# Rounded rows of the split chunks written a second time, into a PSUM bank, in the first gather of a two-layer graph network

## The chip, the cores and the metric

The kernel runs on one core of one Trainium2 chip. The metric is the device time of one execution in microseconds. The core's engines work in parallel, each on its own list of instructions: TensorE (PE), VectorE (DVE), ScalarE (ACT), GpSimd (POOL) and SyncE (SP). They are ordered among each other only by semaphores.

## The reference, cut to what matters

Two graph layers with residual and layer norm over 6,250 nodes of 512 features, with 100,000 edges sorted by destination. Layer 0 is the one that the change touches:

```python
agg = segment_sum(x[src], dst, num_segments=N)     # 6250 x 512
h = (1.0 + eps) * x + agg
h = relu(batch_norm(h @ W1 + b1, g1, be1))         # 512 -> 1024
h = relu(batch_norm(h @ W2 + b2, g2, be2))         # 1024 -> 512
x = layernorm(x + x + h)
```

Layer 1 gathers again over the same edges, with one weight of 512 x 512. All of it is float32.

## The kernel before, in words

The program has five phases: gather 0 (aggregation and the first product of layer 0), the hidden phase (second product), the rows phase (norms), gather 1, and rows again. The change lies in `gather_phase`, which builds both gathers; `layer` says which.

**The gather.** The edges are 782 chunks of 128. For each chunk GpSimd issues one indirect DMA (line 542) that fetches 128 rows of 512 floats from HBM into one slot of `ring`, which has 34 slots in layer 0. The nodes are 50 tiles of 125, handled as 25 pairs (h is 0 or 1 in a pair). A tile takes a window of 18 chunks; neighbouring windows overlap, so a pair needs 782/25 = 31.3 new chunks. SyncE counts landed chunks into the semaphore `landed` (line 518). GpSimd waits for `used` before it overwrites slots.

**The aggregation.** `scatter` on TensorE multiplies, for each chunk of the window, a 0/1 matrix (`select`, which VectorE compares into being in `selection`) with the rows of the chunk, and adds into the tile's PSUM bank. Ten places of the 18 are "whole": float32 operands, two passes (line 767, two records each). Eight places are "split": ScalarE copies the rows from `ring` into `rows_hi[:, k]` rounded to fp32r (line 854, `high_rows`), VectorE subtracts that from the rows and has the low part `rows_lo[:, k]` (line 638, `low_rows`), and TensorE multiplies both, high (line 752) and low (line 757). k is 0 to 7, and each of the eight has a buffer of its own, so ScalarE may run up to eight rows ahead of VectorE, and both ahead of TensorE. TensorE takes whole and split places alternately. The order of the list is fixed:

```python
order = whole[:1]
for k, p in enumerate(whole[1:]):
    order += [p] + split[k:k + 1]
```

**The semaphores of a split row.** `split_hi` counts finished rows of ScalarE, VectorE waits for it; `split_lo` counts finished low parts, TensorE waits for it; `split_used` counts rows that TensorE has consumed, and ScalarE waits for it before it writes buffer k again.

**The rest of a pair.** VectorE forms `sums` = own rows + PSUM bank once a tile is finished (line 653, `read_sums`). TensorE transposes the sums (`turn`), ScalarE rounds them (line 845, `high_part`), VectorE takes the low part (line 661, `low_part`), and TensorE makes the product with W1 in four pieces (line 795, `product`), pushed in between the places of the next pair's tiles: piece 0 after the ninth place of tile 0, piece 1 behind its last, pieces 2 and 3 after the sixth and twelfth place of tile 1. ScalarE reads each piece out of PSUM (line 865, `read_product`), VectorE takes its statistics (line 669). VectorE's and ScalarE's lists for a pair are written out by hand:

```python
read_sums(v, tiles(pair, 1), 1)
low_rows(v, 0, first[0], 0, 2)
low_part(v)
low_rows(v, 0, first[0], 2, 5)
selection(v, 1, tiles(i, 1), first[1])
low_rows(v, 0, first[0], 5, SPLIT)
read_sums(v, tiles(i, 0), 0)
low_rows(v, 1, first[1], 0, 4)
```

and so on. PSUM has eight banks: 0 and 1 hold the tiles' sums, 2 and 3 the transposed, 4 and 5 the products, 6 `column_ps`, and 7 counts edges in layer 1; in layer 0 it is free after the set-up.

Of the kernel before, what the change touches and what calls it, by code (L numbers as in the profile page):

```python
# [4 lines left out]
F32 = mybir.dt.float32  # L5
F32R = mybir.dt.float32r
# [3 lines left out]
ALU = mybir.AluOpType  # L10
ACT = mybir.ActivationFunctionType
# [359 lines left out]
def gather_phase(nc, z, m, layer):  # L371
# [12 lines left out]
    SPLIT = z.SPLIT[layer]  # L384
    WINDOW = z.WINDOW
    SPLIT_AT, ORDER = z.split_places(layer), z.order(layer)
# [19 lines left out]
    with ExitStack() as ctx:  # L406
# [11 lines left out]
        rows_hi, rows_lo = sb("rows_hi", [P, SPLIT, z.D], F32R), sb("rows_lo", [P, SPLIT, z.D], F32R)  # L418
# [21 lines left out]
        split_hi = sem("split_hi")  # L440
        split_lo = sem("split_lo")
# [26 lines left out]

        turn_ps = m.banks(2, 4)
        prod_ps = m.banks(4, 6)  # L470
        count_ps = m.bank(7)

        def tiles(i, h):
            return 2 * i + h
# [7 lines left out]
        def within(engine, value, most, why):  # L482
            return nc.s_assert_within(engine.snap(value), 0, most, skip_runtime_bounds_check_because=why)

        def of_use(engine, i, groups, g):
            return within(engine, i * groups + g, USES - 1, "i and g count below the pairs and the groups")

        def first_chunk(engine, tile, g):

            first = engine.value_load(m.first[:, bass.ds(tile, 1)], min_val=0, max_val=z.CHUNKS - WINDOW)  # L490
            return within(engine, first + g * z.STRIDE, z.CHUNKS - WINDOW + 1, "first is 0 unless there is but one group")

        def of_chunk(engine, first, place):

            at = within(engine, (first + place) % S * z.D, (S - 1) * z.D, "a slot of the ring")
            return ring[:, bass.ds(at, z.D)]
# [9 lines left out]
        with nc.Block(name=f"gather{layer}") as block:  # L506
# [79 lines left out]
            def _(dve):  # L586
                nc.vector.sem_inc(lo_done, 1)
                nc.vector.sem_inc(stats_done, 1)
                if layer == 0:
                    setup.vector(dve)  # L590
                groups = dve.value_load(m.groups, min_val=1, max_val=z.ALL_GROUPS)
# [43 lines left out]
                def low_rows(v, h, first, a, b):  # L635
                    for k in range(min(a, SPLIT), min(b, SPLIT)):
                        dve.wait_ge(split_hi, SPLIT * (2 * v + h) + k + 1)
                        nc.vector.tensor_tensor(rows_lo[:, k, :], of_chunk(dve, first, SPLIT_AT[k]),  # L638
                                                rows_hi[:, k, :].bitcast(F32), ALU.subtract).then_inc(split_lo, 1)

                def read_sums(reads, tile, h):

# [42 lines left out]
                with dve.Fori(0, z.PAIRS) as i:  # L685
                    with dve.Fori(0, groups) as g:
                        v = of_use(dve, i, groups, g)
                        pair = dve.snap(before, min_val=0, max_val=z.PAIRS - 1)
                        first = [first_chunk(dve, tiles(i, h), g) for h in range(2)]
# [32 lines left out]
            def _(pe):  # L722
# [10 lines left out]
                def agg(h):  # L733
                    return m.bank(h)[0:z.NT, :]
# [6 lines left out]
                def scatter(i, v, g, tile, h):  # L741
                    tile_use = pe.snap(2 * v + h)
                    first = first_chunk(pe, tile, g)

                    begin = pe.snap(i * per_pair + first + 1)
                    pe.wait_ge(sums_done[h], v + 1)
                    pe.wait_ge(select_done[h], 2 * v + 2)
                    for n, p in enumerate(ORDER):
                        if p in SPLIT_AT:
                            k = SPLIT_AT.index(p)  # L750
                            pe.wait_ge(split_lo, SPLIT * tile_use + k + 1)
                            high = nc.tensor.matmul(agg(h), select_r[h][:, k, :], rows_hi[:, k, :], start=False,  # L752
                                                    stop=False, skip_group_check=True)

                            if n % 2:
                                high.then_inc(used, 1)
                            nc.tensor.matmul(agg(h), select_r[h][:, k, :], rows_lo[:, k, :], start=False,  # L757
                                             stop=False, skip_group_check=True).then_inc(split_used, 1)
                        else:
                            if n + 1 == WINDOW and layer == 1:  # L760
                                pe.wait_ge(counted[h], v + 1)
                                for c in range(2):
                                    nc.tensor.matmul(count_ps[0:z.NT, bass.ds(tile, 1)], edge_count[h][:, c, :],
                                                     m.ones[:, 0:1], start=False, stop=c == 1, skip_group_check=True)
                            place = last_place if p + 1 == WINDOW else p
                            pe.wait_ge(landed, begin + place)
                            whole = nc.tensor.matmul(agg(h), select[h][:, WHOLE_AT.index(p), :], of_chunk(pe, first, place),  # L767
                                                     start=False, stop=n + 1 == WINDOW, skip_group_check=True)
                            if n % 2:
                                whole.then_inc(used, 1)  # L770
                        if n + 1 in PRODUCT_AT[h]:
                            product(v, PRODUCT_AT[h][n + 1])
# [36 lines left out]
                with pe.Fori(0, z.PAIRS) as i:  # L809
                    clear(i, 0)  # L810
                    clear(i, 1)
                    with pe.Fori(0, groups) as g:
                        v = of_use(pe, i, groups, g)
                        turn(v)
                        scatter(i, v, g, tiles(i, 0), 0)
                        scatter(i, v, g, tiles(i, 1), 1)
# [6 lines left out]
            def _(act):  # L823
# [26 lines left out]
                def high_rows(i, v, h, first, a, b):  # L850
                    for k in range(min(a, SPLIT), min(b, SPLIT)):
                        act.wait_ge(split_used, SPLIT * (2 * v + h) + k + 1)
                        act.wait_ge(landed, i * per_pair + first + (SPLIT_AT[k] + 1))
                        nc.scalar.activation(rows_hi[:, k, :], of_chunk(act, first, SPLIT_AT[k]), ACT.Copy  # L854
                                             ).then_inc(split_hi, 1)

                def read_product(job, pair, b, store=True):
                    if layer == 0 and b == 0:
# [29 lines left out]
                with act.Fori(0, z.PAIRS) as i:  # L888
                    with act.Fori(0, groups) as g:
                        v = of_use(act, i, groups, g)  # L890
                        pair = act.snap(before, min_val=0, max_val=z.PAIRS - 1)
                        first = [first_chunk(act, tiles(i, h), g) for h in range(2)]
# [478 lines left out]
def gnn_kernel(nc, x, src, dst, eps, w1, b1, g1, be1, w2, b2, g2, be2, w3, b3, g3, be3, out):  # L1371
# [7 lines left out]
    with ExitStack() as ctx:  # L1379
# [54 lines left out]
        with ExitStack() as third:  # L1434
            m.w3_hi = sb("w3_hi", [P, z.KD, z.D], F32R, scope=third)
            m.w3_lo = sb("w3_lo", [P, z.KD, z.D], F32R, scope=third)
            m.stats3 = sb("stats3", [P, z.KD, z.PAIRS * 6], scope=third)
            gather_phase(nc, z, m, 1)
# [22 lines left out]
```

## Time and profile before

| | |
|---|---|
| median of 3 runs | 2598.41 us (2590.33 to 2599.28) |
| profiled execution | 2596.4 us, its span 2594.7 us |
| first gather (tiles) | 42 us to 1060 us of the span |
| second gather (tiles) | 1491 us to 2480 us |
| TensorE busy, share of the span | 2309.4 us, 89% |
| GpSimd busy | 1604.1 us, 62% |
| VectorE busy | 1361.8 us, 52% |
| ScalarE busy | 796.0 us, 31% |
| mean granted TensorE clock | 0.942 of full |

Busy time is the sum of an engine's instructions. TensorE's ends are modelled and include time in which a matmul stands in the pipeline. The share over the span mixes phases: GpSimd has nothing to do from 1053 us to 1400 us, and in both gathers it is the other way round. A group's mean duration and a single row's duration are both used below; "x3" in a row means three like instructions in one stretch, whose time runs from the first start to the last end.

### The profile page before, as it was taken

What the parts mean: (1) busy time and instruction counts of PE and PEld (TensorE: products, weight loads), DVE (VectorE), ACT (ScalarE), POOL (GpSimd) and SP (SyncE); (2) the same over time, 40 slices, a digit from 0 to 9 for tenths busy, and PEclk for the clock granted to TensorE, in tenths of its full rate; (3) what the DMA queues carried; (4) which work ended last, traced back from release to release, by engine and by line L of the source; (5) the groups of instructions that cost most, each with busy time, mean ns of one, the idle gap of its engine ahead of it and who ended that gap; (6) DMA issues with size and microseconds to landing.
All of it is one profiled execution on the core that took longest, in us unless ns stands there. A gap on an engine that the chain in (4) does not pass through costs nothing. (4 is left out here: it accounts for less than half of the span.)

```text
span 2594.7 us, 41691 instructions
## 1 busy us (share of the span) xinstructions
PE 2309.4 (89%) x9657; PEld 1514.8 (58%) x9658; DVE 1361.8 (52%) x2155; ACT 796.0 (31%) x1272; POOL 1604.1 (62%) x1729
## 2 busy tenths in 40 slices
PE   3999999999999999799995299999999999999964
PEld 2666666666666666688884255555555555555544
DVE  5555555555555455433336655545545555554557
ACT  1233333333333333455548411111111111111147
POOL 6777777777777777100002467777777777777712
PEclk9999999999999999899996699999999999999976
DMA  7777777777777777332217767777777777777748
GB/s 254 221 237 241 224 246 237 231 242 218 242 240 231 247 223 248 101 111 93 89 55 228 254 190 219 212 226 217 224 222 213 222 222 215 225 224 215 224 136 286
DMA packets 180571, 545.11 MB, mean 210 GB/s; under 512 B 48787, under 2 KB 51178, under 8 KB 175794
## 3 DMA queue, kind: packets, MB, share of 16 engines
q0 software_dynamic: 125120, 410.09, 53.3%
q1 hardware_dynamic: 33880, 78.23, 10.0%
q10 hardware_dynamic: 21544, 56.48, 6.5%
q8 instruction: 10, 0.16, 0.0%
q14 instruction: 17, 0.14, 0.0%
HBM read 493.06 MB, written 51.62 MB: 210 GB/s over the span
## 5 line engine op out<-in xcount | busy, mean ns | idle before, releaser
L767 PE MATMUL psum<-ring,select 128*125 x2600 | 1272.5, 613 | 12.3 <-issue 8.6
L542 POOL DMA_INDIRECT ring<-x_in,staged x782 | 799.2, 1022 | 249.7 <-issue 223.7
L542 POOL DMA_INDIRECT ring<-x_d,staged x782 | 750.2, 959 | 261.7 <-issue 223.0
L767 PEld LDWEIGHTS psum<-ring,select 128*125 128x125 f32 x2600 | 483.5, 192 | 383.6 <-issue 338.2
L638 DVE TENSOR_TENSOR rows_lo<-ring,rows_hi 128x512 fp32r<-128x512 f32 x500 | 327.5, 688 | 281.2 <-ACT rows_hi L854 279.3
L854 ACT ACTIVATE rows_hi<-ring 128x512 fp32r x500 | 289.4, 623 | 418.2 <-SPq L518 282.1
L795 PE MATMUL psum<-sumsT_hi,w_hi 128*128 128x250 f32 x1248 | 401.1, 321 | 4.3 <-DVE sumsT_lo L661 4.3
L752 PE MATMUL psum<-rows_hi,select_r 128*125 128x512 f32 x500 | 380.9, 762 | 7.1 <-DVE rows_lo L638 3.6
L795 PE MATMUL psum<-sumsT_lo,w_hi 128*128 128x250 f32 x1248 | 350.5, 281 | 0.0
L795 PE MATMUL psum<-sumsT_hi,w_lo 128*128 128x250 f32 x1248 | 348.9, 280 | 0.0
L795 PEld LDWEIGHTS psum<-sumsT_hi,w_hi 128*128 128x128 f32 x1248 | 237.9, 191 | 36.0 <-issue 32.6
L795 PEld LDWEIGHTS psum<-sumsT_lo,w_hi 128*128 128x128 f32 x1248 | 239.2, 192 | 30.9 <-issue 29.9
L795 PEld LDWEIGHTS psum<-sumsT_hi,w_lo 128*128 128x128 f32 x1248 | 239.2, 192 | 0.0
L1268 POOL TENSOR_TENSOR both_r<-six_r 125x5 f32<-125x5 f32 x18 | 3.6, 199 | 377.2 <-DVE six_r L1331 377.2
L649 DVE TENSOR_SCALAR lone<-psum 125x1 f32 (+1 forms) x51 | 8.0, 158 | 420.5 <-PE psum L767 420.5
L868 ACT ACTIVATE h3T<-psum,vecs 128x250 f32 (+1 forms) x104 | 43.1, 465 | 568.8 <-PE psum L795 568.8
L865 ACT ACTIVATE hidden<-psum,vecs 128x250 f32<-128x250 f32 x208 | 86.1, 466 | 388.1 <-PE psum L795 388.0
L632 DVE TENSOR_REDUCE edge_count<-select 128x125 bf16<-128x2000 f32 x51 | 202.3, 3967 | 0.0
L757 PE MATMUL psum<-rows_lo,select_r 128*125 128x512 f32 x500 | 199.2, 398 | 0.0
L752 PEld LDWEIGHTS psum<-rows_hi,select_r 128*125 128x125 f32 x500 | 97.3, 195 | 141.2 <-issue 89.5
L1105 PE MATMUL psum<-act_hi,w_hi 128*128 128x500 f32 (+1 forms) x416 | 159.9, 384 | 11.9 <-DVE act_lo L1063 11.9
L1299 PE MATMUL psum<-ident,normed_r 128*125 128x128 f32 x400 | 89.4, 415 | 83.6 <-ACT normed_r L1221 83.6
(161 smaller groups left out, 2257.0 us busy)
## 6 DMA issues: line engine op xcount, KB each, us to landing
hidden_d<-hidden ACTq DMA_DIRECT2D x25, 1000.0 KB
act_f<-hidden_d SPq DMA_DIRECT2D x24, 1000.0 KB
ring<-x_in,staged POOLq DMA_INDIRECT x782, 3.8
ring<-x_d,staged POOLq DMA_INDIRECT x782, 3.7
own<-x_in ACTq DMA_DIRECT2D x50, 224.0 KB
own_r<-x_in SPq DMA_DIRECT2D x10, 1120.0 KB
own<-x_d ACTq DMA_DIRECT2D x50, 224.0 KB
own_r<-x_d SPq DMA_DIRECT2D x10, 1120.0 KB
```

The source lines that it names most:

```text
L542: nc.gpsimd.indirect_dma_start(slot(s), None, table, bass.IndirectOffsetOnAxis(ap=staged[:, s:s + 1], axis=0)).then_inc(gathered[s], 16)
L632: nc.vector.tensor_reduce(edge_count[h][:, 1, :], select[h][:].rearrange("p k n -> p n k"), AX.X, ALU.add).then_inc(counted[h], 1)
L638: nc.vector.tensor_tensor(rows_lo[:, k, :], of_chunk(dve, first, SPLIT_AT[k]), rows_hi[:, k, :].bitcast(F32), ALU.subtract).then_inc(split ...
L752: high = nc.tensor.matmul(agg(h), select_r[h][:, k, :], rows_hi[:, k, :], start=False, stop=False, skip_group_check=True)
L757: nc.tensor.matmul(agg(h), select_r[h][:, k, :], rows_lo[:, k, :], start=False, stop=False, skip_group_check=True).then_inc(split_used, 1)
L767: whole = nc.tensor.matmul(agg(h), select[h][:, WHOLE_AT.index(p), :], of_chunk(pe, first, place), start=False, stop=n + 1 == WINDOW, skip ...
L795: last = nc.tensor.matmul(out, w[:, k, o * P:(o + 1) * P], s[:, k, :], start=n == 0, stop=n == len(parts) - 1)
L854: nc.scalar.activation(rows_hi[:, k, :], of_chunk(act, first, SPLIT_AT[k]), ACT.Copy).then_inc(split_hi, 1)
L865: nc.scalar.activation(hidden[:, o, :], from_, ACT.Identity, bias=m.b1[:, o:o + 1]).then_inc(out_done, 1)
L868: nc.scalar.activation(m.h3T[:, o, bass.ds(pair * z.W, z.W)], from_, ACT.Relu, bias=m.b3[:, o:o + 1]).then_inc(out_done, 1)
L1105: last = nc.tensor.matmul(out, w[:, f * KK + k, o * P:(o + 1) * P], s[:, 0:pairs, k, :] if pairs == 2 else s[:, 0, k, :], start=f == 0 and ...
L1299: last = nc.tensor.transpose(m.bank(n % BANKS)[0:z.NT, k * P:(k + 1) * P], normed[i % 2][:, k, u, :], m.ident[:])
```

## The change: what it does

In layer 0 ScalarE makes each rounded row twice: once into `rows_hi` as before, and once more, with the same source, into PSUM bank 7 (`high_ps`). VectorE's subtraction takes the rounded rows from bank 7 in place of `rows_hi`. Since there is one bank and not eight, ScalarE now also waits, before each row, until VectorE has done the row before (`split_lo`). That semaphore starts at 1 in both layers, and TensorE's waits on it go up by 1 to match. Layer 1 keeps its instructions.

```diff
         turn_ps = m.banks(2, 4)
         prod_ps = m.banks(4, 6)
-        count_ps = m.bank(7)
+
+        high_ps = count_ps = m.bank(7)
...
                 nc.vector.sem_inc(lo_done, 1)
                 nc.vector.sem_inc(stats_done, 1)
+                nc.vector.sem_inc(split_lo, 1)
...
                         dve.wait_ge(split_hi, SPLIT * (2 * v + h) + k + 1)
-                        nc.vector.tensor_tensor(rows_lo[:, k, :], of_chunk(dve, first, SPLIT_AT[k]),
-                                                rows_hi[:, k, :].bitcast(F32), ALU.subtract).then_inc(split_lo, 1)
+                        high = high_ps if layer == 0 else rows_hi[:, k, :].bitcast(F32)
+                        nc.vector.tensor_tensor(rows_lo[:, k, :], of_chunk(dve, first, SPLIT_AT[k]), high, ALU.subtract
+                                                ).then_inc(split_lo, 1)
...
-                            pe.wait_ge(split_lo, SPLIT * tile_use + k + 1)
+                            pe.wait_ge(split_lo, SPLIT * tile_use + k + 2)
...
                         act.wait_ge(split_used, SPLIT * (2 * v + h) + k + 1)
+                        if layer == 0:
+
+                            act.wait_ge(split_lo, SPLIT * (2 * v + h) + k + 1)
                         act.wait_ge(landed, i * per_pair + first + (SPLIT_AT[k] + 1))
-                        nc.scalar.activation(rows_hi[:, k, :], of_chunk(act, first, SPLIT_AT[k]), ACT.Copy
-                                             ).then_inc(split_hi, 1)
+                        high = nc.scalar.activation(rows_hi[:, k, :], of_chunk(act, first, SPLIT_AT[k]), ACT.Copy)
+                        if layer == 0:
+                            high = nc.scalar.activation(high_ps.bitcast(F32R), of_chunk(act, first, SPLIT_AT[k]), ACT.Copy)
+                        high.then_inc(split_hi, 1)
```

What stands on ScalarE for one split row of layer 0, in the loop over pairs, before the change (names in brackets are the semaphores that the instruction waits for; ISA and REGISTER_ALU rows compute a wait's value or an address):

```order
L852 REGISTER_ALU
L853 REGISTER_ALU [waits gather0_split_used]
L854 ISA [waits gather0_landed]
L854 ACTIVATE rows_hi<-ring 128x512
L859 ISA
```

The same place of ScalarE's list after it:

```order
L855 REGISTER_ALU
L859 REGISTER_ALU [waits gather0_split_lo,gather0_split_used]
L860 ISA [waits gather0_landed]
L860 ACTIVATE rows_hi<-ring 128x512
L862 ACTIVATE psum<-ring 128x512
```

One ACTIVATE per row is added behind the old one, and the row's first wait has a second semaphore. On VectorE the list keeps its length; between the tiles of a pair it reads, before:

```order
L638 TENSOR_TENSOR rows_lo<-ring,rows_hi 128x512
L644 REGISTER_ALU [waits gather0_own_in0]
L645 REGISTER_ALU [waits gather0_used]
L653 SCALAR_TENSOR_TENSOR sums_0<-own_0,self_weight,psum 125x512 [waits gather0_turned]
L637 ISA
L638 ISA [waits gather0_split_hi]
L638 TENSOR_TENSOR rows_lo<-ring,rows_hi 128x512
```

and after, at the same place:

```order
L641 TENSOR_TENSOR rows_lo<-ring,psum 128x512
L647 REGISTER_ALU [waits gather0_own_in0]
L648 REGISTER_ALU [waits gather0_used]
L656 SCALAR_TENSOR_TENSOR sums_0<-own_0,self_weight,psum 125x512 [waits gather0_turned]
L639 ISA
L641 ISA [waits gather0_split_hi]
L641 TENSOR_TENSOR rows_lo<-ring,psum 128x512
```

Nothing is moved on VectorE; only the second operand of the subtraction is another.

## Rows read from the trace of the kernel before

**Rows 1.** Busy tenths of GpSimd in 40 slices of the span, from the page.

```profile
POOL 6777777777777777100002467777777777777712
```

**Rows 2.** Groups of instructions, 88 to 1060 us: count, busy us, mean ns, idle before.

```profile
L542 POOL DMA_INDIRECT ring<-x_in,staged x725 | 742.8, 1025 | 223.0 <-issue 207.5 <-PE psum L767 13.7 <-DMA staged<-src_tab 1.8
...
L638 DVE TENSOR_TENSOR rows_lo<-ring,rows_hi 128x512 fp32r<-128x512 f32 x384 | 251.9, 687 | 264.9 <-ACT rows_hi L854 262.9 <-issue 1.7
...
L854 ACT ACTIVATE rows_hi<-ring 128x512 fp32r x384 | 220.4, 623 | 281.2 <-SPq L518 154.7 <-issue 90.6 <-ACT hidden L865 21.0
...
L661 DVE TENSOR_TENSOR sumsT_lo<-psum,sumsT_hi 128x500 fp32r<-128x500 f32 x48 | 30.2, 670 | 4.4 <-ACT sumsT_hi L845 4.3
...
L845 ACT ACTIVATE sumsT_hi<-psum 128x500 fp32r<-128x500 f32 x48 | 25.5, 583 | 11.2 <-PE psum L781 11.0
```

**Rows 3.** The sums instruction: count, durations, first and last start, 80 to 1070 us.

```profile
L653 DVE SCALAR_TENSOR_TENSOR sums<-own,self_weight,psum x49: 746/747/749, 88.4 to 1060.4; 125x512 f32<-125x512 f32 x49
```

**Rows 4.** The same groups in layer 1, 1600 to 2400 us.

```profile
L542 POOL DMA_INDIRECT ring<-x_d,staged x631 | 604.9, 959 | 195.6 <-issue 179.9 <-PE psum L767 12.7 <-DMA staged<-src_tab 3.0
...
L638 DVE TENSOR_TENSOR rows_lo<-ring,rows_hi 128x512 fp32r<-128x512 f32 x80 | 52.1, 691 | 0.0
```

**Rows 5.** Timeline of GpSimd: start us, duration us, instruction, idle before it.

```profile
604.76 0.95 POOL L542 DMA_INDIRECT ring<-x_in,staged  x1 [0.30 <-PE psum L767]
606.01 1.84 POOL L542 DMA_INDIRECT ring<-x_in,staged  x1 [0.30 <-issue]
...
619.49 1.43 POOL L542 DMA_INDIRECT ring<-x_in,staged  x1 [0.30 <-issue]
...
1052.36 0.95 POOL L542 DMA_INDIRECT ring<-x_in,staged  x1 [0.30 <-issue]
```

**Rows 6.** Timeline of VectorE in one pair.

```profile
605.76 1.27 DVE L638 TENSOR_TENSOR rows_lo<-ring,rows_hi 128x512 fp32r<-128x512 f32 x2
...
612.86 0.75 DVE L653 SCALAR_TENSOR_TENSOR sums<-own,self_weight,psum 125x512 f32<-125x512 f32 x1 [2.90 <-PE psum L767]
...
618.82 1.89 DVE L638 TENSOR_TENSOR rows_lo<-ring,rows_hi 128x512 fp32r<-128x512 f32 x3 [1.16 <-ACT rows_hi L854]
...
623.62 0.68 DVE L638 TENSOR_TENSOR rows_lo<-ring,rows_hi 128x512 fp32r<-128x512 f32 x1
```

**Rows 7.** Who waited for whom, 88 to 1060 us: total us, times, longest us.

```profile
PEld psum L752 <- DVE rows_lo L638: 22.8, 81, 1.3
```

**Rows 8.** Timeline of ScalarE and its queue in the same pair.

```profile
601.80 0.83 ACT L865 ACTIVATE hidden<-psum,vecs 128x250 f32<-128x250 f32 x2 [4.27 <-PE psum L795]
603.02 1.67 ACT L854 ACTIVATE rows_hi<-ring 128x512 fp32r x3 [0.39 <-ACT hidden L865]
...
614.16 1.15 ACT L854 ACTIVATE rows_hi<-ring 128x512 fp32r x2 [4.77 <-issue]
...
616.10 1.55 ACTq L839 DMA_DIRECT2D own<-x_in  x3
617.98 2.19 ACT L854 ACTIVATE rows_hi<-ring 128x512 fp32r x4 [1.58 <-SPq L518]
```

**Rows 9.** Timeline of TensorE without the product's matmuls, same pair.

```profile
604.71 1.02 PE L767 MATMUL psum<-ring,select 128*125 x2
...
608.37 0.40 PE L752 MATMUL psum<-rows_hi,select_r 128*125 128x512 f32 x1
...
608.61 0.39 PE L757 MATMUL psum<-rows_lo,select_r 128*125 128x512 f32 x1
...
608.84 1.02 PE L767 MATMUL psum<-ring,select 128*125 x2
...
611.48 1.02 PE L767 MATMUL psum<-ring,select 128*125 x2
```

**Rows 10.** One pair's stretch: length; busy PE, PEld, DVE, ACT, POOL; granted clock, DMA share, GB/s.

```profile
128.00:169.00 41.00, 39.00 (x180) 26.36 (x179) 21.46 (x38) 13.26 (x26) 31.56 (x32) 0.96 0.78 238
```

## The prediction

> **What bounds the kernel now.** I read the slices first: GpSimd is evenly busy through both gathers and idle between them [rows 1]. Then the groups of the stretch in which layer 0's tiles run. GpSimd issued 725 gathers with a mean of 1.025 us and 223.0 us of idle between them, 0.308 us each [rows 2]; together 1.333 us, and 725 x 1.333 = 966 us of the 972 us in the window. It never really rests: 207.5 us of that idle are "issue", the fixed 0.30 us in front of every row [rows 5]. The last gather starts at 1052.4 us [rows 5], 8 us before the last sums of the phase at 1060.4 us. So GpSimd's issue sets the pace of gather 0. A pair of tiles takes (1060.4 - 88.4)/24 = 40.5 us [rows 3]; TensorE shows 39.00 busy of 41.00 [rows 10], so it is a close second.
>
> The timeline of GpSimd shows what a gather costs: most rows last 0.94 to 0.95 us, some 1.43 or 1.84 [rows 5]. The long ones begin while VectorE is in the subtraction of line 638: 606.01 in 605.76 to 607.03, 619.49 in 618.82 to 620.71 [rows 5, 6]. In layer 1, where a window has two split rows and not eight, the mean is 0.959 us [rows 4]. So in layer 0 about 725 x (1.025 - 0.946) = 57 us of GpSimd's time is lengthening beside that subtraction (0.946 being the usual row).
>
> The Trainium skill, "SBUF — State Buffer", section "Who interferes with whom", says that a VectorE instruction with two SBUF inputs contends with a GpSimd instruction that reads SBUF; the trace agrees. In the same section it infers that `tensor_tensor` does not starve descriptor generation, by which the long rows would not exist and the change could give nothing; there the trace disagrees, 1.84 us against 0.95.
>
> **What the change does, part by part.** Layer 0 has 25 x 16 = 400 split rows.
>
> *Removed:* the second SBUF operand of VectorE's subtraction. If that frees GpSimd wholly, a gather costs 0.946 + 0.308 = 1.254 us, and GpSimd could do a pair in 31.3 x 1.254 = 39.2 us.
>
> *Added:* 400 copies on ScalarE, at 0.62 us each 248 us [rows 2]. ScalarE is busy 13.26 of 41 us in a pair [rows 10]; with 16 x 0.62 more it is at 23. As mere work this is covered by its idle time.
>
> *Added:* the wait. This is the term that decides. With one bank, row k+1 may be written only after VectorE has subtracted row k. Before, VectorE did three rows in 1.89 us [rows 6], because ScalarE had run ahead. Now each row is a handshake, of length h:
> - both copies of ScalarE, back to back: 1.15 us, the row of two such copies [rows 8]. The write into PSUM is not in the trace; below, two starts are never closer than (2.19 - 0.62)/3 = 0.52, so 1.04 for both; above, I allow 0.2 more. I take 1.15, since reading PSUM (583 ns for 500 columns) costs ScalarE about what SBUF does (623 for 512).
> - from ScalarE's end to VectorE's start: ScalarE's first of four ends at 617.98 + 0.62 = 618.60, VectorE starts at 618.82 [rows 6, 8]: 0.22.
> - the subtraction: 0.69. With one operand in PSUM the nearest is line 661, 670 ns for 500 columns [rows 2], no dearer.
> - back from VectorE to ScalarE: no such row. TensorE follows VectorE by some 0.06. ScalarE's own step from a finished DMA issue (616.10 + 1.55 = 617.65) over three address steps to its next start at 617.98 is 0.33 [rows 8]; two of these steps lie behind the new wait. 0.06 + 0.22 = 0.28, taken as 0.30; bounds 0.20 and 0.40.
>
> Sum: h = 1.15 + 0.22 + 0.69 + 0.30 = 2.36 us. Sixteen of them are 37.8 us, which alone is near the pair's 40.5; but in five places of a pair the step from one subtraction to the next is longer than h, because other work lies in it:
> - two selections on VectorE, which lie between two subtractions: the third of the three at 618.82 starts at 620.02, the next one at 623.62 [rows 6]: 3.60 each. ScalarE's next row is ready by then.
> - two tile ends. VectorE's `read_sums` waits for TensorE's last place, and that for the last low part: 0.69 (subtraction) + 0.06 + 1.49 (split pair and whole place, 608.37 to 608.84 + 1.02) [rows 9] + 0.36 (whole place over at 612.50, sums at 612.86) [rows 6, 9] + 0.68 (the sums' 0.75 less the usual overlap) = 3.28 each.
> - one `high_part` with the four DMA issues of `load_own` on ScalarE: from the start of a pair of copies at 614.16 to the next copy at 617.98 [rows 8]: 3.82.
>
> Everything else hides: statistics (1.4 us) and `low_part` fit into the 1.67 us that VectorE idles in each handshake; a `read_product` (1.22 us from start to next copy [rows 8]) fits beside the selections or in ScalarE's idle 1.2 us. The five replace five of the 16:
>
> pair = 11 h + 2 x 3.60 + 2 x 3.28 + 3.82 = 11 h + 17.6 = 26.0 + 17.6 = **43.6 us**.
>
> This loop closes over ScalarE, VectorE and, at tile ends, two places of TensorE; nothing in it waits for GpSimd. It is longer than 40.5, so the pace passes from GpSimd to this loop, and what GpSimd gains becomes idle time (waits on `used`). What is queued behind ScalarE's new wait: the later copies, `high_part`, the reads of the products. TensorE, which waited 22.8 us in the whole window for low rows [rows 7], would wait some 1 us at each split row of tile 0: it uses one per 1.3 us and gets one per 2.36.
>
> 24 periods x (43.6 - 40.5) = +74 us. The first pair and layer 1 I leave as they are (layer 1 has the same instructions). Profiled execution: 2596.4 + 74 = 2670; the median of the runs is 2.0 us above that execution: 2672.
>
> The Trainium skill, "VectorE: DVE Perf Modes", section on the TRN2 errata, charges VectorE 62 cycles more for a PSUM source than for SBUF, 65 ns at 0.96 GHz; by that estimate h grows to 2.43 and the time to about 2689. Line 661 reads PSUM and SBUF in 670 ns and shows none of it, so it stays out of the sum.
>
> **Range.** h from 2.20 (each term at its shorter side: 1.10, 0.20, 0.68, 0.22) to 2.65 (a copy into PSUM 0.15 dearer, return 0.40, the rest a little over) gives pairs of 41.8 to 46.8 and +31 to +151 us: 2629 to 2749. All lower bounds at once (1.04 + 0.20 + 0.67 + 0.20 = 2.11) give 40.8, no change.
>
> **The rivals.**
> - *The release wins (faster).* If h were short, GpSimd's pace would still count, at up to 57 us less; with TensorE near its limit (39 of 41 busy) about 24 x 1.5 = 36 to 57: 2540 to 2562. The deciding point is h = (40.5 - 17.6)/11 = 2.08 for equality and 1.96 for the 39.2 of a free GpSimd. For it: the contention is real. Against: three of four terms are measured and make 2.06 without the return. Only if copies overlap with VectorE's work in a way the loop excludes could it be. Chance 0.07.
> - *No change.* h near 2.08 to 2.15, or the loop's extra waits less than I count. 2590 to 2611. Chance 0.08.
> - *The loop plus a slower TensorE (slower still).* The granted clock is 0.96 in a pair's stretch [rows 10], 1.2 GHz for a part of it and 2.4 GHz for the rest. Waits of 1 us at most split rows may bring more time at 1.2 GHz. The sensitive place is piece 1 of the product: at full clock a piece takes about 2.9 us (605.5 to 608.37 [rows 9]), and ScalarE reads it just as it would start the next copy; at half clock it is 2.9 us late and so are all later rows. +2.9 per pair on top is 24 x 2.9 = 70: 2742. Chance 0.20.
> - *GpSimd isn't relieved* (rows stay at 1.025): 31.3 x 1.333 = 41.7 is still under 43.6, so the time is the forecast's. It is contained in it.
>
> **How the numbers follow.** The forecast, the handshake at h 2.2 to 2.65 with the clock as it is, has 0.65, its own range 2629 to 2749. The range of 2618 to 2745 leaves out the faster rival, most of no change, and the upper part of the clock's case. About 0.5% (13 us) is what a measurement of this kernel can tell from nothing. Faster 0.07; same 0.08; slower 0.85.
>
> **What the profile after should show.** GpSimd's gathers in layer 0 at a mean near 0.95 us, with more idle before them, now for TensorE. ScalarE with 400 more instructions. The subtraction still at 0.68 to 0.69 us, its starts 2.3 to 2.4 us apart inside a run, where they were 0.60. Sums 43 to 44 us apart for a pair. TensorE waiting for `rows_lo` by some 4 to 5 us a pair. Layer 1 unchanged in length. The prediction is wrong if the subtraction's starts are under 2.1 us apart, if ScalarE's write to PSUM is much quicker or dearer than 0.62, or if the clock falls for longer.

## The result: 5.8% slower

| | before | after |
|---|---|---|
| median, same comparison | 2595.23 us | 2746.52 us (2745.96 to 2749.34, 4 runs) |
| ratio to before | | 1.0578, 95% interval 1.056 to 1.0595 |
| profiled span | 2594.7 us | 2744.4 us |
| last sums of gather 0 start at | 1060.4 us | 1212.1 us |
| mean granted TensorE clock | 0.942 | 0.936 |

The sign and the mechanism were those forecast. The size was not: +151 us against +74, and 2746.5 lies 1.5 us outside the stated range of 2618 to 2745. All of it is in gather 0: its last sums come 151.7 us later, and everything behind it takes the same time to within 2 us.

Each ratio below compares a kernel with the kernel before in the same set of runs, and the kernel before took 2590 to 2596 us in some sets and 3067 to 3133 us in others, called slow sets here, for a reason that is not known (the expectations put it down to the chip, but chip 4 of the record shows both).

The sums of the changed kernel, from 80 to 1200 us and to 1230 us (count, durations, first and last start), which answer to [rows 3]:

```profile
L656 DVE SCALAR_TENSOR_TENSOR sums<-own,self_weight,psum x48: 746/748/749, 95.2 to 1190.8; 125x512 f32<-125x512 f32 x48
L656 DVE SCALAR_TENSOR_TENSOR sums<-own,self_weight,psum x49: 746/748/750, 95.2 to 1212.1; 125x512 f32<-125x512 f32 x49
```

(1212.1 - 95.2)/24 = 46.5 us a pair, where it was 40.5. The first sums, too, come 6.8 us later (95.2 against 88.4).

The page's groups of the changed kernel, which answer to [rows 2], for the whole of gather 0 (the L755 row counts both gathers, 400 and 100):

```profile
L543 POOL DMA_INDIRECT ring<-x_in,staged x782 | 740.6, 947 | 426.7 <-issue 216.3
...
L641 DVE TENSOR_TENSOR rows_lo<-ring,psum 128x512 fp32r<-128x512 f32 x400 | 274.5, 686 | 480.1 <-ACT psum L862 480.1
...
L755 PEld LDWEIGHTS psum<-rows_hi,select_r 128*125 128x125 f32 x500 | 96.2, 192 | 281.1 <-DVE rows_lo L641 222.1
...
L862 ACT ACTIVATE psum<-ring 128x512 fp32r x400 | 233.2, 583 | 0.0
```

GpSimd's gathers fell to 947 ns: the lengthening is gone. But its idle time rose to 426.7 us. VectorE now waits 480 us for ScalarE's write into PSUM, and TensorE waits for low rows (next table).

Who waited for whom in the changed kernel, 100 to 1190 us (total us, times, longest us):

```profile
DVE rows_lo L641 <- ACT psum L862: 444.8, 305, 1.8
ACT rows_hi L860 <- DVE rows_lo L641: 262.8, 205, 2.3
...
POOL ring L543 <- PE psum L770: 195.9, 90, 9.1
PEld psum L755 <- DVE rows_lo L641: 180.4, 191, 1.6
...
DVE sums L656 <- issue: 73.9, 23, 3.5
...
DVE local L611 <- issue: 15.1, 23, 0.7
```

The first two rows are the handshake, each engine waiting for the other. The third says that GpSimd waits for TensorE, 195.9 us where it was 13.7 [rows 2]. The fourth is TensorE's wait for low rows, 180.4 us or 7.7 a pair, where 4 to 5 were forecast. The last two were not forecast. 73.9 us in 23 times is 3.2 us a pair in which VectorE stood before its sums and waited for no engine; 15.1 us is 0.66 a pair before a selection.

### The profile page after: what moved, and what is told of

It reads as the page before. It is cut to its first block and busy times, and to the rows that moved or that the text cites. A ratio compares the mean times of both kernels' runs of the same rounds, so it can differ in the third digit from the quotient of the medians.

```text
span 2744.4 us, 42493 instructions
## 1 busy us (share of the span) xinstructions
PE 2355.6 (86%) x9657; PEld 1511.0 (55%) x9658; DVE 1372.9 (50%) x2155; ACT 1008.3 (37%) x1672; POOL 1545.2 (56%) x1729
## 5 line engine op out<-in xcount | busy, mean ns | idle before, releaser
L543 POOL DMA_INDIRECT ring<-x_in,staged x782 | 740.6, 947 | 426.7 <-issue 216.3
L860 ACT ACTIVATE rows_hi<-ring 128x512 fp32r x500 | 312.7, 630 | 737.7 <-DVE rows_lo L641 286.2
L641 DVE TENSOR_TENSOR rows_lo<-ring,psum 128x512 fp32r<-128x512 f32 x400 | 274.5, 686 | 480.1 <-ACT psum L862 480.1
L755 PE MATMUL psum<-rows_hi,select_r 128*125 128x512 f32 x500 | 335.0, 670 | 61.5 <-DVE rows_lo L641 58.0
L755 PEld LDWEIGHTS psum<-rows_hi,select_r 128*125 128x125 f32 x500 | 96.2, 192 | 281.1 <-DVE rows_lo L641 222.1
L862 ACT ACTIVATE psum<-ring 128x512 fp32r x400 | 233.2, 583 | 0.0
```

The source lines that it names most:

```text
L543: nc.gpsimd.indirect_dma_start(slot(s), None, table, bass.IndirectOffsetOnAxis(ap=staged[:, s:s + 1], axis=0)).then_inc(gathered[s], 16)
L860: high = nc.scalar.activation(rows_hi[:, k, :], of_chunk(act, first, SPLIT_AT[k]), ACT.Copy)
L862: high = nc.scalar.activation(high_ps.bitcast(F32R), of_chunk(act, first, SPLIT_AT[k]), ACT.Copy)
```

## Where a pair's 46.8 us go

Timeline of VectorE in the changed kernel, cut from one pair. Where a row shows no idle time before it, VectorE came to it straight from other work:

```profile
609.29 0.69 DVE L641 TENSOR_TENSOR rows_lo<-ring,psum 128x512 fp32r<-128x512 f32 x1 [0.90 <-ACT psum L862]
611.71 0.69 DVE L641 TENSOR_TENSOR rows_lo<-ring,psum 128x512 fp32r<-128x512 f32 x1 [1.73 <-ACT psum L862]
...
614.91 0.69 DVE L641 TENSOR_TENSOR rows_lo<-ring,psum 128x512 fp32r<-128x512 f32 x1 [1.34 <-ACT psum L862]
617.23 0.69 DVE L641 TENSOR_TENSOR rows_lo<-ring,psum 128x512 fp32r<-128x512 f32 x1 [1.63 <-ACT psum L862]
619.53 0.69 DVE L641 TENSOR_TENSOR rows_lo<-ring,psum 128x512 fp32r<-128x512 f32 x1 [1.61 <-ACT psum L862]
...
623.15 0.68 DVE L641 TENSOR_TENSOR rows_lo<-ring,psum 128x512 fp32r<-128x512 f32 x1
...
627.75 0.69 DVE L641 TENSOR_TENSOR rows_lo<-ring,psum 128x512 fp32r<-128x512 f32 x1 [1.62 <-ACT psum L862]
630.21 0.75 DVE L656 SCALAR_TENSOR_TENSOR sums<-own,self_weight,psum 125x512 f32<-125x512 f32 x1 [1.77 <-PE psum L770]
630.88 0.68 DVE L641 TENSOR_TENSOR rows_lo<-ring,psum 128x512 fp32r<-128x512 f32 x1
...
637.79 0.69 DVE L641 TENSOR_TENSOR rows_lo<-ring,psum 128x512 fp32r<-128x512 f32 x1 [1.61 <-ACT psum L862]
639.14 0.30 DVE L611 TENSOR_SCALAR local<-dst_t,tile_bases 128x17 f32 x1 [0.66 <-issue]
...
642.19 0.68 DVE L641 TENSOR_TENSOR rows_lo<-ring,psum 128x512 fp32r<-128x512 f32 x1
...
649.12 0.69 DVE L641 TENSOR_TENSOR rows_lo<-ring,psum 128x512 fp32r<-128x512 f32 x1 [1.63 <-ACT psum L862]
...
654.43 0.75 DVE L656 SCALAR_TENSOR_TENSOR sums<-own,self_weight,psum 125x512 f32<-125x512 f32 x1 [3.33 <-issue]
656.11 0.69 DVE L641 TENSOR_TENSOR rows_lo<-ring,psum 128x512 fp32r<-128x512 f32 x1 [0.93 <-ACT psum L862]
```

From start to start of the subtraction, in us:

| step | forecast | measured |
|---|---|---|
| handshake (617.23 to 619.53), 11 of them | 2.36 | 2.31 |
| first selection (619.53 to 623.15) | 3.60 | 3.62 |
| second selection (637.79 to 642.19) | 3.60 | 4.40 |
| end of tile 0 (627.75 to 630.88) | 3.28 | 3.13 |
| `high_part` (611.71 to 614.91) | 3.82 | 3.20 |
| end of tile 1, over the loop's turn (649.12 to 656.11) | 3.28 | 6.99 |
| a pair | 43.6 | 11 x 2.31 + 21.3 = 46.8 |

The pair shown takes 656.11 - 609.29 = 46.8 us, a little more than the mean of 46.5. What happens in the last step stands in the sequencers' own records: the instructions that load registers, which the profile does not count as busy. They are here with start, duration and end in us (not a view of the profile):

```
650.969 0.903 -> 651.872 Vector TENSOR_LOAD L491
651.125 1.055 -> 652.180 Scalar TENSOR_LOAD L491
652.294 1.496 -> 653.790 Vector TENSOR_LOAD L491
652.564 1.261 -> 653.825 Scalar TENSOR_LOAD L491
654.429 0.747 -> 655.176 Vector SCALAR_TENSOR_TENSOR L656
654.594 0.629 -> 655.223 Scalar ACTIVATE L860
```

At the head of the loop both engines load `first`, the number of a tile's first chunk, for the two tiles of the pair out of SBUF into registers. TensorE's last place of tile 1 ended at 650.43 + 1.02 = 651.45, and by the forecast the sums would have followed at 651.8; they start at 654.43. ScalarE's first copy can't start before its own loads are through either, so the next subtraction waits for it once more (0.93). The step before the second selection holds a load of the same kind, 0.32 us long in VectorE's records.

## The experiments

The edits are shown against the changed kernel, unless the text says otherwise.

**relief_only.** Against the kernel before: VectorE's one SBUF operand less, without copies or handshake. VectorE subtracts a constant that a memset left in bank 7; the low parts are not the reference's.

```diff
-                        if layer == 0:
-                            act.wait_ge(split_lo, SPLIT * (2 * v + h) + k + 1)
...
-                        if layer == 0:
-                            high = nc.scalar.activation(high_ps.bitcast(F32R), of_chunk(act, first, SPLIT_AT[k]), ACT.Copy)
...
+                if layer == 0:
+                    dve.wait_ge(setup.vecs_done, 1)
+                    nc.vector.memset(m.bank(7), 0.0)
```

> The changed kernel without ScalarE's second copy and without its new wait; VectorE subtracts what a memset left in bank 7 (so the low parts are not those of the reference). It asks what VectorE's one SBUF operand less is worth by itself. Theory of the handshake (the new loop between ScalarE and VectorE made all of the +151 us, the second operand relieves GpSimd): gathers of layer 0 at a mean of 0.946 us, pairs at 39 to 39.5 us, 2540 to 2570 us. Rival (GpSimd's gathers aren't what paces layer 0): about 2595 us. Rival (a PSUM operand makes VectorE late): above 2600 us.

In a slow set: 1.0054 (1.0024 to 1.0084). Again:

> relief_only once more, since the chip of its first run took 3070 us for the kernel before, with gathers that landed later, and could not tell the kernels apart. The changed kernel without the second copy and without the new wait; VectorE subtracts what a memset left in bank 7. On a chip where the kernel before takes about 2598 us: theory of the handshake 2540 to 2570 us, gathers at 0.946 us; rival (GpSimd does not pace layer 0) about 2595 us.

Measured: 2598.23 us against 2595.02, ratio 1.0006 (0.9982 to 1.003). GpSimd in relief_only_again, 88 to 1040 us:

```profile
L543 POOL DMA_INDIRECT ring<-x_in,staged x724 | 686.6, 948 | 253.6 <-issue 206.2 <-PE psum L773 47.1 <-DMA staged<-src_tab 0.3
```

The relief is complete (948 ns) and brings nothing beyond 0.3% either way; pairs still take (1059.4 - 88.2)/24 = 40.5 us. The last gather starts at 1026.4 us, 33 us before the last sums, where it was 8: GpSimd ran ahead and nothing followed. The handshake theory was right that this operand is the cause of the long gathers, and wrong about what they are worth. In the kernel before, GpSimd was not what held the pace. The rival's 2595 us is what came. One of the ten runs took 2573.3 us, with a granted clock of 0.951 where the others had 0.939 to 0.943; why isn't known.

**copy_only.** The 400 copies without the handshake.

```diff
-                            act.wait_ge(split_lo, SPLIT * (2 * v + h) + k + 1)
+                            act.wait_ge(split_hi, SPLIT * (2 * v + h) + k)
...
-                        high = high_ps if layer == 0 else rows_hi[:, k, :].bitcast(F32)
+                        high = rows_hi[:, k, :].bitcast(F32)
```

> The changed kernel with the second copy into bank 7, but VectorE subtracts rows_hi as before, and ScalarE waits only for its own previous copy instead of VectorE's subtraction. Theory of the handshake: 400 more copies fit into ScalarE's idle time, pairs at 40.5 to 41 us, 2590 to 2615 us. Rival (the work of the copies itself makes the time): 2680 to 2750 us.

In a slow set. Twice again:

> copy_only on a chip where the kernel before takes about 2595 us: the second copy into bank 7 stays, VectorE subtracts rows_hi as before, and ScalarE waits only for its own previous copy. Theory of the handshake: 400 more copies fit into ScalarE's idle time, 2590 to 2620 us. Rival (the work of the copies itself makes the time): 2680 to 2750 us.

> copy_only on a chip where the kernel before takes about 2595 us: second copy kept, VectorE subtracts rows_hi, ScalarE waits only for its own previous copy. Theory of the handshake: 2590 to 2620 us. Rival (the work of the copies itself): 2680 to 2750 us.

All three fell in slow sets: 1.0078 (1.005 to 1.0105), 1.0043 (1.0012 to 1.0074), 1.0053 (1.002 to 1.0086). There the copies cost 0.4 to 0.8%. There is no run of this kernel beside one of 2590 to 2596 us; psum_first, which has the same copies, bounds their cost there.

**wait_only.** The handshake without the second copy (`rows_hi` is VectorE's operand again).

```diff
-                        high = high_ps if layer == 0 else rows_hi[:, k, :].bitcast(F32)
+                        high = rows_hi[:, k, :].bitcast(F32)
...
-                        if layer == 0:
-                            high = nc.scalar.activation(high_ps.bitcast(F32R), of_chunk(act, first, SPLIT_AT[k]), ACT.Copy)
```

> The changed kernel with its new wait, but without the second copy, and with VectorE subtracting rows_hi. The handshake is then one copy shorter: 2.31 - 0.54 = 1.77 us. Theory of the handshake, with the loop turn counted: 11 x 1.77 + 3.6 + 4.4 + 3.1 + 6.4 + 2.7 = 39.7 us a pair, just under GpSimd's pace of 40.5, so 2590 to 2640 us, VectorE's starts 1.8 us apart in a run. Rival (it is the wait as such, whatever its length): near 2746 us.

In a slow set 1.0086 (1.0055 to 1.0118). Again:

> wait_only once more, for the same reason: the new wait without the second copy, VectorE subtracts rows_hi. Theory of the handshake with h = 1.77 us: 2590 to 2640 us. Rival (the wait as such, whatever its length): near 2746 us.

Measured: 2615.6 us against 2595.02, ratio 1.0082 (1.0065 to 1.0099). A handshake of 1.8 us costs 0.8%, not 5.8. Its pairs take (1081.2 - 89.9)/24 = 41.3 us, where 39.7 were expected from the loop alone. Its gathers stay long, 1018 ns on average.

**psum_first.** All the work of the change, but bank 7 is written first and releases VectorE; `rows_hi` is written beside VectorE's subtraction.

```diff
+                            nc.scalar.activation(high_ps.bitcast(F32R), of_chunk(act, first, SPLIT_AT[k]), ACT.Copy
+                                                 ).then_inc(split_hi, 1)
+                        nc.scalar.activation(rows_hi[:, k, :], of_chunk(act, first, SPLIT_AT[k]), ACT.Copy
+                                             ).then_inc(hi_stored if layer == 0 else split_hi, 1)
...
                             pe.wait_ge(split_lo, SPLIT * tile_use + k + 2)
+                            if layer == 0:
+                                pe.wait_ge(hi_stored, SPLIT * tile_use + k + 1)
```

> The changed kernel with ScalarE's two copies in the other order: bank 7 first, which releases VectorE, then rows_hi, beside VectorE's subtraction; TensorE waits for rows_hi by a semaphore of its own. All the work of the change is kept, only the handshake is shorter: 0.58 + 0.21 + 0.69 + 0.29 = 1.77 us. Theory of the handshake: pairs at 39.5 to 41 us with gathers at 0.946 us, 2565 to 2620 us. Rival (the copies' work or the PSUM operand): near 2746 us.

In a slow set 1.016 (1.0105 to 1.0215). Again:

> psum_first once more, for the same reason: bank 7 is written first and releases VectorE, rows_hi is written beside VectorE's subtraction. All the work of the change, a handshake of 1.77 us. Theory of the handshake: 2565 to 2620 us. Rival (the copies' work or the PSUM operand): near 2746 us.

Measured: 2616.72 us against 2595.02, ratio 1.0082 (1.0065 to 1.0099), 130 us less than the change with the same copies and subtractions. Timeline of VectorE in psum_first_again:

```profile
601.31 0.69 DVE L642 TENSOR_TENSOR rows_lo<-ring,psum 128x512 fp32r<-128x512 f32 x1 [1.10 <-ACT psum L864]
603.10 0.69 DVE L642 TENSOR_TENSOR rows_lo<-ring,psum 128x512 fp32r<-128x512 f32 x1 [1.10 <-ACT psum L864]
```

1.79 us from start to start; a pair takes (1081.2 - 88.6)/24 = 41.4 us. So it is the length of the handshake, not the copies' work and not the PSUM operand: 0.52 us less in each took 46.5 - 41.4 = 5.1 us off a pair, and 11 x 0.52 is 5.7. wait_only_again, with a handshake as short but gathers of 1018 ns, takes the same time as this kernel with gathers of 948 ns: here, too, GpSimd's relief brings nothing.

**early_loads.** The changed kernel, with `first` of the next pair loaded in the middle of the pair and carried in registers.

```diff
-                        first = [first_chunk(dve, tiles(i, h), g) for h in range(2)]
+                        first = known(dve, regs)
...
+                        low_rows(v, 1, first[1], 0, 2)
+                        later = [next_first(dve, v, groups, 0)]
+                        low_rows(v, 1, first[1], 2, 3)
+                        later.append(next_first(dve, v, groups, 1))
+                        low_rows(v, 1, first[1], 3, 4)
...
-                        selection(v + 1, 0, tiles(next_pair, 0),
-                                  first_chunk(dve, tiles(next_pair, 0), dve.snap((v + 1) % groups)))
+                        selection(v + 1, 0, tiles(next_pair, 0), later[0])
...
+                        for h in range(2):
+                            dve.reg_mov(regs[h], later[h])
```

The same on ScalarE, before row 4 of tile 1 and behind it (rows count from 0). The edit stands in both layers.

> The changed kernel, but VectorE and ScalarE read the two values of first for the next pair out of memory in the middle of the pair, beside waits, and carry them over the loop's turn in registers. Nothing else is changed. Theory (the step that the prediction missed is the loop's turn: 3.7 us in which both engines load registers before the first row of a pair, and 0.8 us before the second selection): pairs go from 46.7 to 42.5 to 44 us, 2640 to 2690 us. Rival (those loads lie beside TensorE's lateness and cost nothing): 2740 to 2750 us.

Measured: 2649.61 us, ratio to before 1.0212 (1.0195 to 1.0229), 97 us less than the change. The last sums of gather 0 start at 1114.1 us, 98 us earlier. Timeline of VectorE:

```profile
642.52 0.69 DVE L654 TENSOR_TENSOR rows_lo<-ring,psum 128x512 fp32r<-128x512 f32 x1 [1.63 <-ACT psum L881]
645.08 0.75 DVE L669 SCALAR_TENSOR_TENSOR sums<-own,self_weight,psum 125x512 f32<-125x512 f32 x1 [0.58 <-PE psum L789]
646.38 0.69 DVE L654 TENSOR_TENSOR rows_lo<-ring,psum 128x512 fp32r<-128x512 f32 x1 [0.56 <-ACT psum L881]
...
674.60 0.69 DVE L654 TENSOR_TENSOR rows_lo<-ring,psum 128x512 fp32r<-128x512 f32 x1 [1.62 <-ACT psum L881]
678.19 0.68 DVE L654 TENSOR_TENSOR rows_lo<-ring,psum 128x512 fp32r<-128x512 f32 x1
```

The turn's step is 3.86 us and not 6.99, the second selection's 3.59 and not 4.40. A pair takes (1114.1 - 91.3)/24 = 42.6 us. The other steps stay, the handshake at 2.30 and the end of tile 0 at 3.12; only `high_part` is shorter too, 2.93 for 3.20. The missing step is shown: with it undone the changed kernel comes to 2650 us, inside the stated range. That is less than the 2672 forecast, since a few other terms of the sum were too long.

**early_loads_before.** The same edit in the kernel before.

> The kernel before, with only the early loads of the next pair's first. Theory of two near limits in layer 0 (GpSimd's issue, 1.33 us a gather, and TensorE's own work with the wait at the loop's turn): GpSimd keeps its pace, so 2580 to 2597 us, gathers still at a mean of 1.02 us or more. Rival (the loop's turn alone paces the kernel before): 2530 to 2570 us.

In a slow set 0.9845 (0.9795 to 0.9895). Again:

> The kernel before with only the early loads, again, since the chip of its first run took 3073 us for the kernel before; there it was 1.5% faster. Theory of two near limits: GpSimd keeps its pace, 2580 to 2597 us, gathers still at a mean of 1.02 us or more. Rival (the loop's turn alone paces the kernel before): 2530 to 2570 us.

A slow set once more, 0.9915 (0.9878 to 0.9953). And a third time:

> The kernel before with only the early loads, where the kernel before takes about 2595 us. Theory of two near limits: GpSimd keeps its pace, 2580 to 2597 us, gathers at a mean of 1.02 us or more. Rival (the loop's turn alone paces the kernel before): 2530 to 2570 us.

Measured: 2573.87 us against 2590.6, ratio 0.9929 (0.9911 to 0.9947). That is below the 2580 to 2597 of the theory and above the rival's 2530 to 2570, and the gathers mean 1.000 us, not 1.02. Sums of early_before_third, first from 88 to 740 us, then from 740 to 1060 us:

```profile
L666 DVE SCALAR_TENSOR_TENSOR sums<-own,self_weight,psum x33: 746/747/749, 104.7 to 730.2; 125x512 f32<-125x512 f32 x33
L666 DVE SCALAR_TENSOR_TENSOR sums<-own,self_weight,psum x15: 746/748/749, 752.4 to 1039.3; 125x512 f32<-125x512 f32 x15
```

(730.2 - 104.7)/16 = 39.1 us a pair, most of them 38.7; then (1039.3 - 752.4)/7 = 41.0. The stretch from 200 to 900 us, first in the kernel before, then here (columns as in [rows 10]):

```profile
200.00:900.00 700.00, 664.77 (x3085) 452.94 (x3084) 373.17 (x661) 234.16 (x452) 539.75 (x527) 0.97 0.77 236
```

```profile
200.00:900.00 700.00, 666.05 (x3133) 450.85 (x3131) 379.24 (x666) 241.96 (x459) 536.32 (x538) 1.00 0.80 241
```

The granted clock is 1.00 and not 0.97. In the kernel before it fell to 1.2 GHz for 3.4 us behind the turn of most pairs, 41 us of these 700 in all; here 7 us of the 700 are at 1.2 GHz. GpSimd in the last seven pairs:

```profile
L555 POOL DMA_INDIRECT ring<-x_in,staged x225 | 225.3, 1001 | 68.5 <-issue 64.3 <-PE psum L786 4.0 <-DMA staged<-src_tab 0.3
```

A gather with its idle time takes (225.3 + 68.5)/225 = 1.306 us, and 31.3 of them 40.9 us, the 41.0 of these pairs. GpSimd waits for TensorE in only 4.0 us of 300, and ScalarE's wait for landed rows rises from 80.2 us in the 652 before to 134.3 in these 300. So GpSimd holds the last seven pairs. Until then it had lived off its lead, the 34 slots of the ring that it fills ahead of the tiles, and at 39.1 us a pair the lead shrinks by some 1.7 us a pair (estimate, 40.8 less 39.1). In the kernel before the turn's wait, with the clock that it costs, held the pace at 40.5 us. GpSimd alone would have needed 31.3 x 1.333 = 41.7, but there its lead lasted to the end: its last gather started 8 us before the last sums. Easing the turn brought 0.7%, easing GpSimd alone nothing.

**psum_first with early loads.** The shorter handshake and the early loads, the whole computation.

> Bank 7 written first (handshake 1.77 us) together with the early loads; the whole computation. The loop of ScalarE and VectorE is then 42.6 - 11 x 0.54 = 36.7 us a pair, under TensorE's work and GpSimd's 39.1. Theory: pairs at 39 to 40 us, 2550 to 2590 us, faster than the kernel before. Rival (the ScalarE work of two copies a row or another wait keeps it there): 2600 to 2620 us.

In a slow set 0.9985 (0.9957 to 1.0012). Twice again:

> Bank 7 written first together with the early loads, again, for the same reason. Theory: the loop of ScalarE and VectorE at 36.7 us a pair lies under TensorE's work and GpSimd's 39.1, pairs at 39 to 40 us, 2550 to 2590 us. Rival: 2600 to 2620 us.

> Bank 7 written first together with the early loads, on the same chip. Theory: pairs at 39 to 40 us, 2550 to 2590 us. Rival: 2600 to 2620 us.

The second fell in a slow set once more, 0.9983 (0.9954 to 1.0011). The third took 2581.51 us against 2590.6, ratio 0.995 (0.9929 to 0.9971). Better than the kernel before, not better than early_before_third. Its pairs take (1044.7 - 89.1)/24 = 39.8 us with gathers at 945 ns: GpSimd is relieved, and TensorE waits 87.9 us for low rows:

```profile
PEld psum L777 <- DVE rows_lo L655: 87.9, 120, 1.0
```

From the second pair on every pair takes 39.8 or 39.9 us and the granted clock stays at full, while GpSimd waits for TensorE 32.8 us in 952. That speaks for the handshake as the limit here, even at 1.8 us; the 36.7 us a pair that had been expected of its loop were too few. The PSUM operand gives GpSimd room that its own price takes away.

**Both limits eased.** Two kernels, both in slow sets alone, and so without a clear answer. relief_early_loads has no handshake (relief_only with early loads; low parts not the reference's):

> relief_only (no second copy, no new wait, VectorE subtracts what a memset left in bank 7, so the low parts are not those of the reference) with the early loads. Both limits are eased at once. Theory of two near limits: pairs at 39 to 39.6 us, 2550 to 2575 us, though neither edit alone gave more than 0.6%. Rival (a third limit, TensorE's work alone, is already at 40.5): about 2595 us.

0.9921 (0.9885 to 0.9957). The kernel before with early loads alone had 0.9845 and 0.9915 in slow sets, so no gain of the relief shows there, but in that trace GpSimd waits for TensorE 234 us in 1162 and is no limit at all. psum_first_early, in the same set as this kernel, had 0.9985: the copies and the short handshake together cost 0.6% there. And every_second_early, the whole computation, in which only the rows with odd k go through bank 7, so that a handshake covers two rows:

```diff
-                        high = high_ps if layer == 0 else rows_hi[:, k, :].bitcast(F32)
+                        high = high_ps if layer == 0 and k % 2 else rows_hi[:, k, :].bitcast(F32)
...
-                            act.wait_ge(split_lo, SPLIT * (2 * v + h) + k + 1)
+                            act.wait_ge(split_lo, SPLIT * (2 * v + h) + k)
```

> The changed kernel with early loads, but only every second split row (k odd) goes through bank 7; the others are subtracted from rows_hi. ScalarE waits for VectorE's subtraction of two rows before, so a handshake of 2.31 us covers two rows, 1.16 a row, less than TensorE's 1.32. GpSimd is relieved of about half of its lengthening. Theory (the kernel before has three limits close together: GpSimd's issue over the whole layer, TensorE's own 38.7 us a pair, and the wait at the loop's turn, which also lets TensorE's clock fall): pairs at 38.7 us nearly throughout, gathers at a mean of 0.97 to 0.99 us, 2545 to 2572 us where the kernel before takes about 2595 us. Rival (half the relief is not enough, or ScalarE's coupling costs it): 2573 to 2590 us, as early_before_third and psum_first_early_third.

0.9931 (0.989 to 0.9972), its gathers at a mean of 971 ns, as expected. Whether 38.7 us a pair can be held to the end stays open; by estimate, 24 x (40.5 - 38.7) = 43 us off the 2595 would make some 2550 us.

## Why the prediction was wrong in size

- *GpSimd's issue sets the pace of gather 0*: wrong. relief_only_again shows 0 us for its relief where I had put up to 57. GpSimd works without a pause, but its own 31.3 x 1.333 = 41.7 us a pair is more than the 40.5 that a pair takes, and that is possible only while it lives off its lead. That it worked all the time didn't show that the others waited for it. It was the next limit (early_before_third). The sum did not rest on it, the faster rival did: relief alone left the time at 2598, so the rival's 2540 to 2562 us could not have come even with a free handshake.
- *The change takes the lengthening from the gathers*: right, 1025 to 947 ns.
- *h = 2.36 us*: right, 2.31. The copy into PSUM takes 583 ns, not 620; the return from VectorE to ScalarE about 0.30 (620.22 to 620.51). The subtraction with its PSUM operand takes 686 ns, where it was 687. The Trainium skill, "VectorE: DVE Perf Modes", section on the TRN2 errata, charges 62 cycles more for a PSUM source; these rows show none of it.
- *Pair = 11 h + 17.6*: this is the step that failed, in the constant. "Two tile ends, 3.28 each" treated tile 1's end as tile 0's. Behind tile 1 lies the turn of the loop, and the register loads of both engines stand there: 6.99 us, +3.7 a pair. Together with the second selection (+0.8, a load of the same kind), `high_part` (-0.6), tile 0's end (-0.15) and the handshake (-0.55) it is +3.2 in the pair shown, which is 0.3 longer than the mean. Over all pairs the miss is 24 x (46.5 - 43.6) = 70 us. Another 6.8 us lie ahead of the first sums, where the prediction left the first pair as it was (early_loads has 2.9 of them left, with its first sums at 91.3). Together they are the 77 us by which +151 exceeds +74. early_loads removes the loads at the turn and before the selection and lands at 2650.
- The row that showed it was there and I passed over it: ScalarE's two copies at 614.16 had stood 4.77 us idle before them with "issue" as the releaser [rows 8], and VectorE's sums at 612.86 were followed by a subtraction only at 615.19. In the kernel before the loads lay beside TensorE's last places of tile 1 and cost less. I used the duration of that row and not its idle time.
- *Slower TensorE by its clock*: part of it came, but it is not the cause. From 200 to 900 us TensorE's clock stood at 1.2 GHz for 75 us, where it was 41. The falls begin at the turn, within 2.4 us of the sums there, where TensorE has just stood still (3.77 us before 655.23), and not at piece 1 of the product as the rival had it. In early_loads only 10 us of these 700 are at 1.2 GHz, and the steps away from the turn and the second selection are the same but for 0.3 us of `high_part`. That the rival's price, 2742 us, is near the result is luck.
- *Chances and range*: slower at 0.85 was right. The forecast's own range of 2629 to 2749 does hold 2746.5, but that is luck as well: its upper end stands for a handshake of 2.65 us, and the handshake was 2.31.

## What to carry to other kernels

A buffer that goes from eight places to one turns two engines that ran apart into one loop; its length is both engines' instructions plus two semaphore steps, here 2.31 us a row against 0.60, and it must be set against what the consumer needs per row (1.3 us) before anything that the change relieves is counted. When such a loop is added up, the turn of the program's loop belongs in it: idle time put down to "issue" at a loop's head is a cost that a tighter coupling will lay open. And the relief of an engine that is busy all the time is worth nothing while another wait holds the pace: here GpSimd, at work all the time, came second to the wait at the loop's turn, because the ring gave it a lead.

## What was not expected of the hardware

- In the sequencers' records from 100 to 1000 us, loading a value from SBUF into a register took 0.32 us on VectorE before a selection, and 0.5 to 1.5 us at the loop's head of the changed kernel, where ScalarE loads as well (0.6 to 1.7 us). With the loads moved to the middle of the pair (early_loads) it took 0.30 us on VectorE and 0.3 to 0.5 on ScalarE. Why it is longer at the loop's head wasn't tested.
- The second SBUF operand of VectorE's subtraction lengthens GpSimd's indirect DMA instruction: 1025 ns on average with it, 947 to 948 ns without, in four kernels. With the handshake and the SBUF operand (wait_only_again) it is 1018.
- With the early loads in the kernel before, TensorE's granted clock from 200 to 900 us rose from 0.97 to 1.00.
